# Gate logits of an eight-expert router: 64 narrow matmuls over H's blocks in place of 16 wide ones, their copy and 8 turns

## The reference

```python
logits = jnp.einsum('bsh,he->bse', hidden_states, gate_w)        # hidden 512, 8 experts
routing_weights, selected_experts = jax.lax.top_k(logits, K)     # K = 2
h = jax.nn.relu(jnp.einsum('bsh,hi->bsi', hidden_states, up_w)) ** 2
shared_out = jnp.einsum('bsi,ih->bsh', h, down_w)
x_latent = jnp.einsum('bsh,hl->bsl', hidden_states, fc1_w)
expert_out = jnp.einsum('bsl,lm->bsm', x_latent, expert_w)
moe_out = expert_out * jnp.sum(routing_weights, axis=-1, keepdims=True)
routed_out = jnp.einsum('bsl,lh->bsh', moe_out, fc2_w)
return _layernorm(shared_out + routed_out, ln_gamma, ln_beta)
```

## Time and profile before

| | us |
|---|---|
| median of 3 runs (lowest, highest) | 217.63 (217.41, 219.53) |
| the profiled execution, whole | 217.47 |
| its span, first to last instruction | 215.7 |
| PE busy | 211.2 |
| PE weight loads busy | 183.5 |
| DVE busy | 123.5 |
| ACT busy | 79.7 |
| POOL busy | 61.7 |

### The profile page before, as it was taken

One profiled execution on the slowest core, in us unless ns is written; L12 is line 12 of the kernel. 1 busy time (PEld: TensorE's weight loads), 2 busy tenths in 40 slices (PEclk: granted clock), 3 DMA queues, 4 the chain that ended last, 5 costly groups with the idle time before them and its releaser, 6 DMA issues.

```text
span 215.7 us, 3111 instructions
## 1 busy us (share of the span) xinstructions
PE 211.2 (98%) x1159; PEld 183.5 (85%) x1159; DVE 123.5 (57%) x265; ACT 79.7 (37%) x154; POOL 61.7 (29%) x77
## 2 busy tenths in 40 slices
PE   7999999999999999999999999999999999999994
PEld 7998778888887789987888888888998998999984
DVE  4994366869535455597762034456996537435443
ACT  6975755369384612222222034431013112121110
POOL 3045421340475620021960012442264202202000
PEclk9999999999999999999999999999999999999999
DMA  6999655420000000174444000000000110110104
GB/s 173 331 410 404 231 111 102 67 37 0 0 3 0 0 0 3 25 125 68 92 39 146 0 0 0 3 0 2 0 3 0 49 49 3 49 50 0 52 0 146
DMA packets 31455, 14.94 MB, mean 69 GB/s; under 512 B 25336, under 2 KB 26168, under 8 KB 31440
## 3 DMA queue, kind: packets, MB, share of 16 engines
q1 hardware_dynamic: 30624, 14.05, 23.2%
q10 hardware_dynamic: 816, 0.69, 1.1%
HBM read 12.62 MB, written 2.11 MB: 68 GB/s over the span
## 4 chain that ended last, share of the span: by engine, by line
PE 92%; DVE 4%; DMA 1%; issue 0%; ACT 0%; DVEq 0%
PE PS L1215 26%; PE PS L1217 25%; PE PS L1216 25%; PE PS L1232 9%; PE PS L1340 3%; DVE XS L448 2%; DVE H_lo L885 1%; DMA wc_nat<-in_L_cond_weight_dram 1%; PE PS L1257 1%; PE PS L1256 1%; PE PS L1369 0%; PE PS L1266 0%; DVE wc_pad L973 0%; ACT H_hi L662 0%; DVE up_lo L864 0%
## 5 line engine op out<-in xcount | busy, mean ns | idle before, releaser
L910 DVE TENSOR_TENSOR PS<-PS,relu 128x512 f32<-128x512 f32 x16 | 11.2, 699 | 30.5 <-ACT relu L675 30.5
L1215 PE MATMUL PS<-H_hi,up_hi 128*128 128x512 f32 x64 | 25.6, 400 | 0.4 <-DVE H_lo L885 0.4
L1217 PE MATMUL PS<-H_hi,up_lo 128*128 128x512 f32 x64 | 25.0, 390 | 0.0
L1216 PE MATMUL PS<-H_lo,up_hi 128*128 128x512 f32 x64 | 25.0, 390 | 0.0
L1232 PE MATMUL PS<-wconv,XS 128*128 128x128 f32 x192 | 22.4, 276 | 0.2
L1232 PEld LDWEIGHTS PS<-wconv,XS 128*128 128x128 f32 x192 | 21.9, 192 | 0.7 <-ACT wconv L643 0.2
L1217 PE MATMUL PS<-qkT_hi,H_lo 128*128 128x320 f32 x64 | 19.8, 309 | 0.0
L1216 PE MATMUL PS<-qkT_lo,H_hi 128*128 128x320 f32 x64 | 19.8, 309 | 0.0
L1215 PE MATMUL PS<-qkT_hi,H_hi 128*128 128x320 f32 x64 | 19.7, 308 | 0.0
L675 ACT ACTIVATE relu<-PS 128x512 f32<-128x512 f32 x16 | 9.5, 594 | 24.8 <-PE PS L1217 22.4
L595 POOL TENSOR_TENSOR X<-X,rowb 128x512 f32<-128x512 f32 x8 | 10.3, 1293 | 28.1 <-PE PS L1340 28.1
(11 more groups left out here) (187 smaller groups left out, 457.9 us busy)
## 6 DMA issues: line engine op xcount, KB each, us to landing
up_raw<-in_L_ffn_up_w_dram SPq DMA_DIRECT2D x2, 1024.0 KB, 8.6
dn_raw<-in_L_ffn_down_w_dram SPq DMA_DIRECT2D x2, 1024.0 KB, 13.8
out_dram<-X SPq DMA_DIRECT2D x7, 256.0 KB, 2.0
X<-in_x_dram SPq DMA_DIRECT2D x1, 1024.0 KB, 14.5
XS<-in_L_ffn_W_dram SPq DMA_DIRECT2D x16, 64.0 KB, 2.2
X<-in_x_dram SPq DMA_DIRECT2D x2, 256.0 KB, 3.0
X<-in_x_dram SPq DMA_DIRECT2D x1, 512.0 KB, 5.2
fc<-in_L_ffn_fc_w_dram SPq DMA_DIRECT2D x1, 512.0 KB, 5.7
```

What stands on the lines that cost most here:

```text
L910: nc.vector.tensor_tensor(U[i % 2], U[i % 2], relu[:], ALU.mult).then_inc(s_sq, 1)
L1215: nc.tensor.matmul(o, lh, rh, start=start, stop=False)
L1216: nc.tensor.matmul(o, lh, rl, start=False, stop=False)
L1217: return nc.tensor.matmul(o, ll, rh, start=False, stop=stop)
```

## The change

The logits are computed with the operands exchanged. For each of the four tiles of 128 tokens, each of the four hidden blocks and each part of H, a block of 128x128 of H is loaded as weights and 16 columns of gate_hl (8 high, 8 low) are streamed past it, into the tile's 16 columns of M[1]: tokens come out on the partitions at once. So 32 passes a half stand at the place of `gate_rows`, and the copy on ACT, the four transposes behind `up(1)`, the zero columns of gate_hl and their memset on POOL, and three semaphores are gone. A spare tile keeps the addresses of what follows in SBUF. `gate_sum` and all that follows it is as it was.

```diff
-        gate_hl = sb("gate_hl", [P, PH, P], F32R)
+        gate_hl = sb("gate_hl", [P, PH, 2 * NE], F32R)
+        sb("spare2", [P, PH, P - 2 * NE])
...
-            nc.gpsimd.memset(gate_hl[:].bitcast(mybir.dt.uint32), 0).then_inc(s_gatez, 1)
...
-            def gate_copy(h):
-                act.wait_ge(s_gT, h + 1)
-                if h:
-                    act.wait_ge(s_gp, h)
-                else:
-                    act.wait_ge(s_fc2, 1)
-                nc.scalar.activation(glog, M[0][0:2 * NE, :], ACT.Copy).then_inc(s_gTs, 1)
...
                 up_relu(i0)
-                if h == 0:
-                    gate_copy(h)
-                    up_split(i0)
-                else:
-                    up_split(i0)
-                    gate_copy(h)
+                up_split(i0)
                 up_relu(i0 + 1)
...
-            def gate_rows(h):
+            def gate_logits(h):
 
                 if h == 0:
                     pe.wait_ge(s_gate, 1)
                 else:
-                    pe.wait_ge(s_tf, 3)
-                for p in range(PH):
-                    nc.tensor.matmul(M[0], gate_hl[:, p], H_hi[:, p], start=(p == 0), stop=False)
-                    last = nc.tensor.matmul(M[0], gate_hl[:, p], H_lo[:, p], start=False, stop=(p == PH - 1))
-                last.then_inc(s_gT, 1)
-
-            def gate_logits(h):
-
-                pe.wait_ge(s_gTs, h + 1)
-                if h:
                     pe.wait_ge(s_tf, TPH)
                 for t in range(TPH):
-                    last = nc.tensor.transpose(M[1][:, t * 2 * NE:(t + 1) * 2 * NE],
-                                               glog[:, t * P:(t + 1) * P], ident[0:2 * NE, 0:2 * NE])
+                    ts = slice(t * P, (t + 1) * P)
+                    for p in range(PH):
+                        nc.tensor.matmul(M[1][:, t * 2 * NE:(t + 1) * 2 * NE], H_hi[:, p, ts], gate_hl[:, p],
+                                         start=(p == 0), stop=False)
+                        last = nc.tensor.matmul(M[1][:, t * 2 * NE:(t + 1) * 2 * NE], H_lo[:, p, ts], gate_hl[:, p],
+                                                start=False, stop=(p == PH - 1))
                 last.then_inc(s_gp, 1)
...
@@ latent
-                else:
-                    pe.wait_ge(s_gTs, h + 1)
+                elif h:
+                    pe.wait_ge(s_tf, 3)
...
                 up(h * IC)
-                gate_rows(h)
+                gate_logits(h)
                 up(h * IC + 1)
-                gate_logits(h)
                 up(h * IC + 2)
```

More of the change, by code:

```diff
@@ L218, in bass_adaln_ffn @@
         cond = fc2[:].rearrange("p c l -> p (c l)")
-        glog = cond[0:2 * NE, 512:512 + TOKH]
         W0, W1, W2 = cond[:, 0:CHID], cond[:, CHID:2 * CHID], cond[:, 256:256 + KE]
@@ L317, in bass_adaln_ffn @@
         s_H = sem("s_H")
-        s_gatez = sem("s_gatez")
         s_gateh = sem("s_gateh")
@@ L321, in bass_adaln_ffn @@
         s_logit = sem("s_logit")
-        s_gT = sem("s_gT")
-        s_gTs = sem("s_gTs")
         s_gp = sem("s_gp")
@@ L723, in _ @@
             act.wait_ge(ld_gate, 16)
-            act.wait_ge(s_gatez, 1)
             nc.scalar.activation(gate_hl[:, :, 0:NE], gate[:], ACT.Copy).then_inc(s_gateh, 1)
```

## The result

The changed kernel takes 225.38 us (median of 4, 223.47 to 226.51) against 217.69 us of the kernel before: a ratio of 1.0325, 95% interval 1.028 to 1.037. It is slower by 3.3%, where +1.1% was forecast as the likeliest. The profiled execution took 223.47 us with a span of 221.7.

A forecast was written before the change was run, and what follows sets the result against it. PE's list was taken to bound the kernel from the gate on. Per half 3.68 us comes and 2.35 goes, +1.33, so +2.65 in all on the profiled 217.47 gives 220.1 us; range 219.0 to 223.3.

The forecast's parts named there:

- What bounds the kernel: From the gate's first pass to the end, PE's list sets the time; any change in its length moves the end equally.
- What goes: Gate, per half: eight wide passes (1.81 us) and the four turns (0.54 us) leave PE, 2.35 us.
- What comes: Gate, per half: 32 passes of 16 columns, pitch set by the load of H, 0.115 us each, 3.68 us.
- 32-column pair: Conditioning's plain float32 passes at L1465: following loads start 0.11 us apart, taken as the nearest row for a narrow pass.
- main case: Gate's narrow passes at a pitch of 0.11 to 0.12 us, no stall: 219.8 to 220.5 us, chance 0.68.
- the sum: Gate passes added minus PE work removed: 3.68 - 2.35 = +1.33 us a half, +2.65 us in all.
- What moves with it: Behind the gate: up(1) and the store of sums 1.87 us later, all from up(2) 1.33 later, nothing stalls.
- the slack: First half, from lat_lo done to the start of routed: 1.27 us, forecast to shrink by 0.54 to 0.73.
- The clock falls: Each gate stretch drops PE to 1.2 GHz over some 3 us of dense work: +5.7 us, 223.1, chance 0.12.
- The other rivals: Gate's narrow passes: faster loads, 216.7 us at a 0.061 pitch, chance 0.12; two loads each, 226.8 us, chance 0.08.

The follow-up runs named there:

- run with 128 columns: Changed kernel with gate_hl padded with zeros to 128 columns, all streamed in each of the 32 passes a half; 220.12 us, ratio 1.012.
- two groups: Changed kernel with each half's 32 narrow passes split into two groups of 16, the second behind up(1); 221.58 us, ratio 1.0163.
- interleaved kernel: Changed kernel with each half's 32 narrow passes dealt out singly, two or three behind each wide pass of up(1); 221.25 us, ratio 1.0166.

## Why the prediction was wrong

The direction was right and the size was not; 225.38 us lies above the range (219.0 to 223.3).

- **What bounds the kernel** held: PE's list is the time. Every stretch without the gate is the same to 0.04 us in all kernels with the old addresses.
- **What goes**, 8 x 0.2266 + 0.54 = 2.35 us a half: the turns measured 0.62 by the version without them, 0.08 more than I read. The stretches with 32 and with 16 narrow passes (+1.20 and -0.58) together give 2.36 for what goes; where the 0.07 between the two lies is open.
- **What comes**, 32 x 0.115: measured 32 x 0.1116 = 3.57, near the row of the 32-column pair (0.11) and not midway to 0.12. The 13 ns that a wide pass costs over its stream do not show on top of a load. 3.57 - 2.355 = 1.2 a half fits the measured 1.20. The run with 128 columns, in which the clock holds, took 220.12 us against the main case's 220.1; the mechanism is the forecast one, but the agreement to the tenth is luck, since its stretches are 2 x 1.20 = 2.40 longer and the sum had 2.65.
- **What moves with it**: no wait came up, as forecast, but the slack did not shrink to 0.73. The run with 128 columns, where the clock holds, can be compared with the earlier trace rows. Before (two rows) and with 128 columns (three rows):

```profile
30.87 0.17 DVE L906 TENSOR_TENSOR ssum<-top 128x4 f32<-128x4 f32 x1
31.07 0.39 ACTq L686 DMA_DIRECT2D sum_rows<-ssum  x1
```

```profile
31.78 0.36 ACTq L684 DMA_DIRECT2D sum_rows<-ssum  x1
...
45.38 0.69 DVE L910 TENSOR_TENSOR lat_lo<-PS,lat_hi 128x512 fp32r<-128x512 f32 x1 [0.67 <-ACT lat_hi L695]
...
47.89 0.39 PE L1200 MATMUL PS<-ex_hi,lat_hi 128*128 128x512 f32 x1
```

  lat_lo is done at 46.07 and `routed` starts at 47.89: the slack grew from 1.27 to 1.82. Before, the store started as DVE finished ssum (31.04), and not behind `up_relu(1)`, as the forecast had it; with the sums ready sooner it moved by 0.71 (31.07 to 31.78) instead of 1.87.
- **The step that failed** is the chance of 0.12 for "The clock falls", and with it the main case, whose sum has no term for the clock. In the profiled execution the granted clock fell behind each gate stretch, at 1.6 us a fall. The argument against it was that the convolution loads weights as often for longer without a fall. The convolution streams 128 columns under each load, and so does the run with 128 columns, which holds the clock; the loads were the wrong likeness. The rival's own sentence, that the array streams 7 ns in each 115, was the fact that counted. The Trainium skill, page "TensorE: Matmul & The Clock Gate", section "Part 1: The HAM clock gate", ties the high clock to how busy the array is; the runs at 16 and 128 columns don't contradict it, but the profile's busy share for PE is full in both and doesn't tell the two apart.
- **The size of that rival**, +5.7 us, came close for the profiled execution (223.1 forecast, 223.47 measured), in part by luck: measured were 2 x 1.20 for the loads, where the sum had 2 x 1.33, 2 x 1.6 for the clock, where it had 2 x 1.5, and 0.37 in the opening, where it had nothing. It was too small for the median. I priced each fall at 3 us of dense work, a length that no row of before gives; three of the four executions had a mean clock of 0.976 or 0.977, a third unit of low clock, which is another 1.6 us. And the sum had no term for the opening, though one of the three runs of before had taken 219.53 us against 217.41; it added 0.37 here and 2.10 in the second trace of the changed kernel.
- **The other rivals** fell: no load in the narrow passes lasts less than 187 ns, and there are 64 records for 64 calls, so no second load.

## What to carry to other kernels

Exchanging the operands so that the small one is streamed makes the number of weight loads the price: 0.111 us each here against 0.227 for a whole pass of 512 columns, so it pays only under 2.36 / 0.111 = 21 passes a half. If a run of load-bound passes is needed, stream more columns (zeros are free up to 128 here) or put wide passes between: 16 columns in each 0.11 us for 3.6 us brought PE to 1.2 GHz for the next 3.3 to 6.5 us, which cost more (1.6 or 3.2 us) than the loads did (1.2). And hold every tile's address when a small tile changes, or an experiment measures the addresses.

## What the runs showed of the hardware that I had not expected

- **Addresses.** 384 bytes of shift in SBUF, from gamma and H_hi on, make a pass of 512 columns take 0.2323 us instead of 0.2267, 2.5% more, and the span 2.5 us longer (219.8 - 215.7, less 1.6 in the opening). The median is 4.1 us above the kernel before, so it overstates the addresses. It shows in passes that stream the moved H_hi over the unmoved fc_hi (the latents, 0.2325) as much as in those that stream the unmoved dn_hi and dn_lo over the moved ring (0.2328 against 0.2271), and in the rest of the span up to the queries. So neither the streamed operand alone nor the loaded one alone has to be the moved one. The last stage, from the first query pass to the last pass, took 61.89 us with 384 bytes and 61.90 before, but 62.40 with the further shift to an odd multiple of 32. Which step of address matters, and why, was not tried.
- **The opening.** The first `up` started between 22.2 and 24.4 us, in kernels that have the same passes on PE ahead of it. These are weight loads of the two groups, which began late, over the same instructions as those of the interleaved kernel, which did not:

```profile
4.40 1.35 PEld L1389 LDWEIGHTS PS<-ident,wc_pad 64*128 64x128 f32 x12 [0.23 <-issue]
5.97 0.93 PEld L1379 LDWEIGHTS PS<-ones 128*128 128x128 f32 x4
6.78 4.35 PEld L1214 LDWEIGHTS PS<-wconv,XS 128*128 128x128 f32 x24
```

```profile
4.40 0.92 PEld L1414 LDWEIGHTS PS<-ident,wc_pad 64*128 64x128 f32 x12 [0.23 <-issue]
5.46 0.52 PEld L1404 LDWEIGHTS PS<-ones 128*128 128x128 f32 x4
6.23 2.75 PEld L1214 LDWEIGHTS PS<-wconv,XS 128*128 128x128 f32 x24 [0.26 <-ACT wconv L639]
```

  24 loads of the first convolution took 4.35 us in the one and 2.75 in the other. The median of a load's record is 333 ns in the one and 192 in the other, and 333 is also what loads last at a granted clock of 0.50 in the changed kernel. So it looks like the low level again, but the granted clock says 1.00 there in both, and no row shows it. The kernel before has such a spread too: of 23 executions, 12 took 217.4 to 218.0 us and 11 took 218.9 to 219.6. Medians of four executions here can be off by some 2 us for it, and the readings above rest on stretches of the trace beside them.
- **One fall, two lengths.** The low clock lasted 3.3 or 6.5 us behind the same passes, with dense work under it all the time. The longer one was seen in one trace.
